# Attention kernel: row maxima split in transposed form, the high part of the turned rows on ScalarE, the lowest part of v on GpSimd, the maxima sent by SyncE

## The chip, the cores and the metric

The kernel runs on one core of a Trainium2 chip. That core has five engines with a program each: TensorE (PE, matmuls into PSUM), VectorE (DVE), ScalarE (ACT), GpSimd (POOL) and SyncE (SP, which here only issues DMAs). They wait for each other through semaphores. The metric is the device time of one execution in microseconds (us).

## The reference

For 8 batches of 512 tokens with 512 channels and 16 heads of 32:

```python
mod = (silu(c) @ wmod).reshape(8, 6, 1, -1)          # sa, ca, ga, sb, cb, gb
h = layernorm(x) * (1 + ca) + sa
q, k, v = split(h @ W_attn.T)                        # heads of 32
att = softmax(causal(q @ k.T) / sqrt(32)) @ v
x = x + ga * (att @ W_proj.T)
h = layernorm(x) * (1 + cb) + sb
x = x + gb * mlp(h)                                  # 512 -> 1024 -> 1024 -> 512, relu
```

## The kernel before, in words

`setup` computes the modulation, `attention` the softmax part for all batches, `mlp` the projection and the MLP. The change is in `attention` alone.

Full fp32 accuracy comes from split numbers: a value is written as a high part and a remainder, and three products of parts are added. So q and k have two parts each (`qk_parts`), h has two (`h_parts`), v three in bf16 (`v_parts`: columns D:2D high, 2D:3D middle, 0:D lowest).

**Slots and units.** The work of a batch is 8 slots (one per pair of heads, numbered 0 to 7), and a slot has 5 units (u = 0 to 4). In slot p all stages of different pairs run side by side, each some slots behind (`behind(b, p, lag, first)`; a lag beyond slot 0 falls into the next batch's first slots):
- lag 0: PE computes the scores of pair p by query (L758), DVE takes the row maxima (L653, L657);
- lag 1: the maxima of the pair before are transposed by PE in unit 1 (L808) and sent by DMA into two rows of `stack`, the operand of the second score matmuls;
- lag 2: PE computes the scores again, by key, with the maximum subtracted through those two rows (L770); ACT takes the exponential twice, to f16 (L529) and to f32 (L536); POOL (units 0, 1, 3, 4) and DVE (unit 2, L668) form the low part `prob_lo`;
- lag 3: PE multiplies with v (L790), DVE gathers (L639, L642);
- lag 4: POOL scales (L465), SP stores `o_rows` in odd slots (L424).

The first key matmul of a slot (unit 0) waits for `max_in` of its pair: the maxima that were turned one slot earlier have to be in `stack`.

**The linear work of the next batch** is dealt out over the units by the table WORK, from slot 4 of one batch to slot 3 of the next: four transposes of x (TURN, slot 4, units 0 to 3), eight q/k projections (QK 0 to 7), eight v units. QK 1 ends in slot 5 unit 4, QK 3 in slot 7 unit 0, QK 5 in slot 1 unit 3, QK 7 in slot 2 unit 4. After each of these four SP issues 12 DMAs of 128 KB, which lay `qk_parts` out into `stack` (L398, a "group" below). Two PSUM banks alternate over all linear units; `lin_act` counts what ACT has taken from them and `lin_taken` what DVE has taken.

**Order.** Each engine's order is fixed by the code: one in-order stream per engine, `slot(b, p, ...)` for each slot, batch 0 and batch 7 written out and batches 1 to 6 in a loop. On ACT, a unit is: exponentials, then in unit 1 the copy of the turned maxima (L543) and their two DMA issues (L546), then the linear item. On SP: linear item's group, then (unit 1, odd slots) the store.

**The maxima before.** DVE forms -max rounded to fp32r (L676, `neg_max[..., 0, :]`) and its remainder (L679) at the end of the slot, on 128 x 8 elements; PE turns both at once into 16 rows of 128; ACT copies these 16 rows to `max_rows` (two buffers) and issues two DMAs of 4 KB.

Of the kernel before, what the change touches and what calls it, by code (L numbers as in the profile page):

```python
# [294 lines left out]
def attention(nc, mem, x, wqkv, ident, mask_qk, mask_kq, ident_bf, mod_cols, attn_dram):  # L295
# [16 lines left out]
    neg_max = mem.sb("neg_max", [P, 2, 2, 2 * NT])  # L312
    max_rows = mem.sb("max_rows", [4 * NT, 2, P], F32R)
# [13 lines left out]
    lin_done, lin_act, h_hi, lin_taken = (mem.sem(n) for n in ("lin_done", "lin_act", "h_hi", "lin_taken"))  # L327
    v_mid_ready, v_split = (mem.sem(n) for n in ("v_mid_ready", "v_split"))
    stack_in = [mem.sem(f"stack_in{g}") for g in range(GROUPS)]
    score_done, score_taken, max_hi, max_ready, turn_done, turn_taken = (  # L330
        mem.sem(n) for n in ("score_done", "score_taken", "max_hi", "max_ready", "turn_done", "turn_taken"))
# [16 lines left out]
    def v_no(n, g, t):  # L348

        return V_UNITS * n + NT * g + t  # L350

# [31 lines left out]
    with nc.Block() as block:  # L383
        @block.sync
        def _(sp):
# [46 lines left out]
        def _(pool):  # L432
# [15 lines left out]

            def slot(b, p, first, more):
                for u in range(UNITS):  # L450
# [18 lines left out]
                    if p == 2 and u == 4 and more:  # L469
                        inverse_deviation(b + 1)  # L470
# [4 lines left out]
        def _(act):  # L475
            act.sem_inc(prob_ready, KEY_CREDITS)
            act.sem_inc(turn_taken, 1)

            def modulate(n, c):
# [39 lines left out]
            def slot(b, p, first, more):  # L519
                for u in range(UNITS):  # L520
# [18 lines left out]
                    if u == 1 and turned:  # L539

                        n, q = turned
                        act.wait_ge(turn_done, PAIRS * n + q + 1)
                        nc.scalar.copy(max_rows[:, q % 2, :], turn_bank[0:4 * NT, 0:P]).then_inc(turn_taken, 1)  # L543
                        act.wait_ge(turn_taken, 1 + PAIRS * n + q + 1)
                        for part in range(2):
                            act.dma_start(  # L546
                                f32(stack[3 * D + part:3 * D + part + 1, 0, 2 * q:2 * q + 2, :]),
                                f32(max_rows[2 * NT * part:2 * NT * (part + 1), q % 2, :]))\
                                .then_inc(max_in[q], 16)
# [6 lines left out]
        def _(dve):  # L556
# [38 lines left out]
            def v_rest(n, g, t):  # L595

                hs = slice(g * H // 2, (g + 1) * H // 2)
                dve.wait_ge(v_split, V_CREDITS + v_no(n, g, t) - 1)
# [3 lines left out]

            def v_lowest(n, g, t):
                hs = slice(g * H // 2, (g + 1) * H // 2)
                rest = heads(full[:, ORDER.index((V, g, t)) % 2, 0:C // 2])
                dve.wait_ge(v_mid_ready, v_no(n, g, t) + 1)
                nc.vector.tensor_tensor(v[:, t, hs, 0:D], rest, v[:, t, hs, 2 * D:3 * D],
                                        ALU.subtract).then_inc(v_split, 1)
# [12 lines left out]
            def step_after_item(n, item):  # L621

                if item[0] == V and last_item(item):
                    v_lowest(n, item[1], item[2])

# [3 lines left out]
            for item in before_first():  # L629
                after_item(0, item)  # L630
                step_after_item(0, item)
# [12 lines left out]
            def slot(b, p, first, more):  # L644
                for u in range(UNITS):
# [14 lines left out]
                    if not (first and p == u == 0):  # L660
                        earlier = (work(b, p, u - 1, more) if u else work(b, p - 1, UNITS - 1, more) if p
                                   else [(b, item) for item in WORK[PAIRS - 1][UNITS - 1]])
                        for n, item in earlier:
                            step_after_item(n, item)
# [7 lines left out]
                    if p < PAIRS and u == UNITS - 1:  # L672

                        dve.wait_ge(score_taken, SCORE_CREDITS + unit_no(b, p, UNITS))
                        peak = row_max[:, p % 2].rearrange("p h t -> p (h t)")
                        nc.vector.tensor_scalar_mul(neg_max[:, p % 2, 0, :].bitcast(F32R), peak, -1.0)\  # L676
                            .then_inc(max_hi, 1)
                        dve.wait_ge(max_hi, PAIRS * b + p + 1)
# [14 lines left out]
        def _(pe):  # L693
# [69 lines left out]
            def scores_by_key(b, p, u):  # L763

                bank = key_bank[(UNITS * p + u) % 2]
                if u == 0:
                    pe.wait_ge(max_in[p], 32 * (b + 1))
# [27 lines left out]
            def slot(b, p, first, more):  # L795
                for u in range(UNITS):
# [469 lines left out]
```

## Time and profile before

| | |
|---|---|
| time, median of 3 runs | 1666.01 us (1664.12 to 1668.75) |
| the profiled execution | 1668.86 us, its span 1667.1 us, mean granted PE clock 0.972 |
| busy: PE, DVE, ACT, POOL | 1536.4 us (92%), 1000.6 (60%), 644.2 (39%), 370.6 (22%) |
| attention | from about 60 to 780 us |
| MLP | from about 780 us to the end |

Shares are over the whole span and average two parts with different limits. In the profile, L12 is line 12 of the kernel; SPq and ACTq are the DMA issues of these engines, with the time that an issue occupies them. The granted clock is a fraction of 2.4 GHz. Idle time of an engine is put down to what ended it.

### The profile page before, as it was taken

The page shows a single profiled execution, that of the slowest core. Times are in us where ns is not written, and L with a number is a line of the kernel's source. Part 1 is how long each engine was busy: PE and PEld are TensorE (multiplying, and loading weights), DVE is VectorE, ACT ScalarE, POOL GpSimd, SP SyncE. Part 2 cuts the span into 40 slices and gives each one's busy share as a digit, 9 for nine tenths or more (in the row PEclk, how much of TensorE's full clock was granted, in tenths as well). Part 3 has the DMA queues.
Part 4 walks back from the last instruction along what each step waited for, and adds up shares of the span by engine and source line. Part 5 has one row for each costly group of instructions (what it writes and reads, how often), then busy time and mean ns, then how long its engine had stood idle before and what let it go on. Part 6 is the DMA issues. An engine that isn't in the chain of part 4 may idle for free.

```text
span 1667.1 us, 33396 instructions
## 1 busy us (share of the span) xinstructions
PE 1536.4 (92%) x12032; PEld 1345.7 (81%) x12032; DVE 1000.6 (60%) x2287; ACT 644.2 (39%) x1346; POOL 370.6 (22%) x360
## 2 busy tenths in 40 slices
PE   5499989898989898985699999999999999999998
PEld 1377777787777777874699999999999999999998
DVE  2477878878788878773844444445444454444442
ACT  2146666666666666674512122121212122121211
POOL 0224555454555554553000000000000000000000
PEclk9699999999999999996799999999999999999999
DMA  5162534243425252423600111001100011011100
GB/s 227 43 162 62 127 73 123 71 120 76 121 69 134 58 135 62 110 71 112 204 26 20 45 45 45 13 31 44 44 30 27 31 44 44 0 51 37 44 14 13
DMA packets 75272, 116.98 MB, mean 70 GB/s; under 512 B 10568, under 2 KB 27976, under 8 KB 74704
## 3 DMA queue, kind: packets, MB, share of 16 engines
q1 hardware_dynamic: 68816, 107.31, 23.4%
q10 hardware_dynamic: 6400, 8.92, 1.5%
q8 instruction: 36, 0.59, 0.1%
q14 instruction: 20, 0.16, 0.0%
HBM read 48.52 MB, written 16.81 MB: 39 GB/s over the span
## 4 chain that ended last, share of the span: by engine, by line
PE 51%; DVE 1%; DMA 1%; SPq 0%; ACT 0%; issue 0%; POOL 0%; DVEq 0%; POOLq 0%
PE feature L1203 33%; PE token L1184 16%; PE feature L1174 1%; PE token L1165 1%; DVE w L1115 1%; DMA b_rows<-b 0%; DMA w_ring<-wproj_t 0%; DVE y L1069 0%; SPq L945 0%; DVE y L1067 0%; ACT w L1021 0%; DVE attn_tiles L1093 0%; POOL mlp_rstd L982 0%; DVE gated L1077 0%; DVE res_tiles L1080 0%
## 5 line engine op out<-in xcount | busy, mean ns | idle before, releaser
L454 POOL TENSOR_TENSOR prob_lo<-prob,prob_hi 128x512 f16<-128x512 f32 x256 | 302.0, 1183 | 362.0 <-ACT prob L536 361.0
L1203 PE MATMUL feature<-y,w 128*128 128x256 f32 x3072 | 377.5, 284 | 5.1 <-DVE w L1115 5.1
L1203 PEld LDWEIGHTS feature<-y,w 128*128 128x128 f32 x3072 | 374.2, 190 | 6.7 <-DVE w L1115 5.3
L1015 ACT ACTIVATE mlp_full<-feature,b_cols 128x256 f32<-128x256 f32 x256 | 120.4, 476 | 647.0 <-PE feature L1203 617.4
L1067 DVE CAST y<-mlp_full 128x256 fp32r<-128x256 f32 x256 | 75.2, 294 | 302.4 <-ACT mlp_full L1015 302.1
L529 ACT ACTIVATE prob_hi<-key_score 128x512 f16<-128x512 f32 x320 | 192.3, 601 | 143.0 <-PE key_score L770 140.9
L708 PE MATMUL lin<-h_parts,wqkv 128*128 128x512 f32 x768 | 215.1, 403 | 9.5 <-DVE h_parts L585 9.5
L1203 PEld LDWEIGHTS feature<-turned,w 128*128 128x128 f32 x1536 | 189.2, 191 | 5.1 <-DVE w L1115 3.8
L1203 PE MATMUL feature<-turned,w 128*128 128x256 f32 x1536 | 189.7, 284 | 3.4 <-DVE turned L1069 3.4
L536 ACT ACTIVATE prob<-key_score 128x512 f32<-128x512 f32 x320 | 192.4, 601 | 0.0
L982 POOL TENSOR_TENSOR mlp_rstd<-mlp_var_eps,mlp_minus_half 128x2 f32<-128x2 f32 x16 | 11.1, 696 | 799.3 <-DVE mlp_var_eps L1088 799.3
L1184 PE MATMUL token<-w,y 128*128 128x512 f32 x768 | 183.6, 398 | 0.0
L657 DVE TENSOR_REDUCE row_max<-score 128x1 f32<-128x512 f32 (+2 forms) x384 | 181.0, 501 | 3.5 <-PE score L758 3.3
L1184 PEld LDWEIGHTS token<-w,y 128*128 128x128 f32 x768 | 143.4, 188 | 33.7
L708 PEld LDWEIGHTS lin<-h_parts,wqkv 128*128 128x128 f32 x768 | 140.2, 192 | 36.6 <-DVE h_parts L585 11.4
L758 PE MATMUL score<-stack 96*128 96x512 f32 (+3 forms) x512 | 155.0, 364 | 2.4 <-DMA stack<-qk_parts 2.4
L770 PE MATMUL key_score<-stack 98*128 98x512 f32 (+3 forms) x512 | 142.9, 341 | 0.0
L790 PEld LDWEIGHTS o_bank<-v_parts,prob_hi 128*128 128x128 f16 x1280 | 100.5, 99 | 27.4 <-issue 23.2
L790 PE MATMUL o_bank<-v_parts,prob_hi 128*128 128x97 bf16 x1280 | 117.4, 212 | 4.3 <-POOL prob_lo L454 2.8
L790 PE MATMUL o_bank<-v_parts,prob_lo 128*128 128x65 bf16 x1280 | 114.5, 196 | 0.0
L1069 DVE TENSOR_TENSOR y<-mlp_full,y 128x256 fp32r<-128x256 f32 x256 | 109.0, 426 | 8.8
L716 PE MATMUL lin<-wqkv,h_parts 128*128 128x256 f32 x768 | 107.7, 285 | 0.0
(95 smaller groups left out, 1902.8 us busy)
## 6 DMA issues: line engine op xcount, KB each, us to landing
stack<-qk_parts SPq DMA_DIRECT2D x384, 128.0 KB, 2.4
x_tiles<-x SPq DMA_DIRECT2D x32, 256.0 KB, 3.1
attn_dram<-o_rows SPq DMA_DIRECT2D x32, 256.0 KB, 2.2
attn_tiles<-attn_dram SPq DMA_DIRECT2D x16, 512.0 KB, 4.4
res_tiles<-x SPq DMA_DIRECT2D x16, 512.0 KB, 3.6
out<-res_tiles ACTq DMA_DIRECT2D x16, 512.0 KB, 2.8
wmod_sb<-wmod SPq DMA_DIRECT2D x4, 1536.0 KB, 16.4
w_ring<-w_t SPq DMA_DIRECT2D x12, 512.0 KB, 6.2
```

Of the source, the lines that this page charges most:

```text
L454: nc.gpsimd.tensor_tensor(prob_lo[:, key[1] % 2, u, :], prob[:, u, :], prob_hi[:, key[1] % 2, u, :], ALU.subtract).then_inc(lo_pool, 1)
L529: nc.scalar.activation(prob_hi[:, q % 2, u, :], bank[:], ACT.Exp, scale=SOFTMAX_SCALE, bias=P_SHIFT)
L536: nc.scalar.activation(prob[:, u, :], bank[:], ACT.Exp, scale=SOFTMAX_SCALE, bias=P_SHIFT)\
L657: last = nc.vector.reduce_max(row_max[:, p % 2, hh, t:t + 1], bank[:, col:col + P * (t + 1)], AX.X)
L708: mm = nc.tensor.matmul(lin_bank_of((QK, f))[:], wqkv[:, wl, c, at:at + P], h[:, hl, c, :], start=(c == 0 and k == 0), stop=(c == NC_ - 1 ...
L758: mm = nc.tensor.matmul(bank[:, col:col + n], stack[0:3 * D, 0, head, t * P:(t + 1) * P], stack[0:3 * D, 1, head, 0:n], start=False, stop= ...
L770: mm = nc.tensor.matmul(bank[:, col:col + n], stack[0:3 * D + 2, 1, head, t * P:(t + 1) * P], stack[0:3 * D + 2, 0, head, t * P:T], start= ...
L790: mm = nc.tensor.matmul(o_bank[:, i * VW + low:(i + 1) * VW], part[:, p % 2, u, at:at + P], v[:, j, head, low:VW], start=(j == 0 and part ...
L1015: nc.scalar.activation(full[:, f % 2, :], fbank[f % 4][:, 0:CH], ACT.Relu, bias=bias[:, f:f + 1])\
L1069: nc.vector.tensor_tensor(dst[:, 1, c, :], full[:, ring, :], f32(dst[:, 0, c, :]), ALU.subtract)\
L1184: mm = nc.tensor.matmul(bank[:], data[:, dl, c, t * P:(t + 1) * P], weights[:, wl, c, :], start=(c == 0 and i == 0), stop=(c == chunks - 1 ...
L1203: mm = nc.tensor.matmul(fbank[f % 4][:, 0:CH], weights[:, wl, c, f * P:(f + 1) * P], data[:, dl, c, :], start=(c == 0 and i == 0), stop=(c ...
```

## The change

- **Maxima.** PE turns the plain maxima (8 rows) as soon as `score_taken` allows. ACT writes the negated, rounded rows (`max_rows[:, 0, :]`), DVE forms the remainder from the same PSUM bank in unit 2, after its prob_lo and its linear item, into `max_rows[:, 1, :]`. SP issues the two DMAs in unit 2. `max_rows` has one buffer, so ACT waits for the DMAs of the pair before.
- **Turned rows of h.** ACT applies the modulation twice, to `full` and, as fp32r, to the high part of `h_parts`; the cast on DVE goes. The PSUM bank is then free after ACT, and PE's wait is changed to `lin_act` where the bank's last user was a TURN.
- **v.** The lowest part is computed by POOL, right after the linear item's unit, and no longer by DVE one unit later. DVE's next use of the `full` buffer waits for it.

```diff
         @block.sync (in slot, each unit)
                     for n, item in work(b, p, u, more):
                         after_item(n, item)
+                    turned = behind(b, p, 1, first)
+                    if u == 2 and turned:
+                        n, q = turned
+                        wait_apart(sp, turn_taken, 1 + PAIRS * n + q + 1, (o_out[0], 16))
+                        for part in range(2):
+                            sp.dma_start(f32(stack[3 * D + part:3 * D + part + 1, 0, 2 * q:2 * q + 2, :]),
+                                         f32(max_rows[:, part, :])).then_inc(max_in[q], 16)
                     done = behind(b, p, 4, first)
...
         @block.gpsimd
+            def v_lowest(n, item):
+                if item[0] != V or not last_item(item):
+                    return
+                g, t = item[1:3]
...
+                pool.wait_ge(v_mid_ready, v_no(n, g, t) + 1)
+                nc.gpsimd.tensor_tensor(v[:, t, hs, 0:D], rest, v[:, t, hs, 2 * D:3 * D], ALU.subtract)\
+                    .then_inc(v_split, 1)
...
+                    for n, item in work(b, p, u, more):
+                        v_lowest(n, item)
                     if p == 2 and u == 4 and more:
...
         @block.scalar
-                nc.scalar.activation(full[:, c % 2, :], lin_bank_of((TURN, c))[:], ACT.Identity,
-                                     scale=mod_now[:, NC_ + c:NC_ + c + 1], bias=mod_now[:, c:c + 1])\
-                    .then_inc(lin_act, 1)
+                if c >= 2:
+                    act.wait_ge(lin_taken, LIN_CREDITS + lin_no(n, (TURN, c - 2)) + 1)
+                for made in (full[:, c % 2, :], h[:, 0, c, :]):
+                    last = nc.scalar.activation(made, lin_bank_of((TURN, c))[:], ACT.Identity,
+                                                scale=mod_now[:, NC_ + c:NC_ + c + 1], bias=mod_now[:, c:c + 1])
+                last.then_inc(lin_act, 1)
...
                         act.wait_ge(turn_done, PAIRS * n + q + 1)
-                        nc.scalar.copy(max_rows[:, q % 2, :], turn_bank[0:4 * NT, 0:P]).then_inc(turn_taken, 1)
-                        act.wait_ge(turn_taken, 1 + PAIRS * n + q + 1)
-                        for part in range(2):
-                            act.dma_start(
...
+                        act.wait_ge(max_in[(q - 1) % PAIRS], 32 * (n + 1 if q else n))
+                        nc.scalar.activation(max_rows[:, 0, :], turn_bank[0:2 * NT, 0:P], ACT.Copy, scale=-1.0)\
+                            .then_inc(max_hi, 1)
...
         @block.vector
             def split_h(n, c):
-                nc.vector.tensor_copy(h[:, 0, c, :], full[:, c % 2, :]).then_inc(h_hi, 1)
-                dve.wait_ge(h_hi, NC_ * n + c + 1)
...
-            def v_lowest(n, g, t):
...
-                        nc.vector.tensor_scalar_mul(neg_max[:, p % 2, 0, :].bitcast(F32R), peak, -1.0)\
...
+                    turned = behind(b, p, 1, first)
+                    if u == 2 and turned:
+
+                        n, q = turned
+                        dve.wait_ge(max_hi, PAIRS * n + q + 1)
                         nc.vector.scalar_tensor_tensor(
-                            out=neg_max[:, p % 2, 1, :].bitcast(F32R), in0=peak, scalar=-1.0,
-                            in1=neg_max[:, p % 2, 0, :], op0=ALU.mult, op1=ALU.subtract).then_inc(max_ready, 1)
+                            out=max_rows[:, 1, :], in0=turn_bank[0:2 * NT, 0:P], scalar=-1.0,
+                            in1=f32(max_rows[:, 0, :]), op0=ALU.mult, op1=ALU.subtract).then_inc(turn_taken, 1)
...
         @block.tensor
-                    pe.wait_ge(lin_taken, lin_no(n, unit_of(item)) + 1)
+                    place = ORDER.index(unit_of(item))
+                    if ORDER[place - 2][0] == TURN:
+                        pe.wait_ge(lin_act, lin_no(n, unit_of(item)) - 1)
+                    else:
+                        pe.wait_ge(lin_taken, lin_no(n, unit_of(item)) + 1)
...
-                        pe.wait_ge(max_ready, PAIRS * n + q + 1)
+                        pe.wait_ge(score_taken, SCORE_CREDITS + unit_no(n, q, UNITS))
                         pe.wait_ge(turn_taken, PAIRS * n + q + 1)
-                        nc.tensor.transpose(turn_bank[0:4 * NT, 0:P],
-                                            neg_max[:, q % 2, :, :].rearrange("p l m -> p (l m)"), ident[:])\
+                        nc.tensor.transpose(turn_bank[0:2 * NT, 0:P],
+                                            row_max[:, q % 2].rearrange("p h t -> p (h t)"), ident[:])\
                             .then_inc(turn_done, 1)
```

SP's order before, in the loop, from the group of QK 1 (end of slot 5) to the store of slot 7:

```order
L398 DMA stack<-qk_parts 32x2x512 [waits lin_taken]
L398 DMA stack<-qk_parts 32x2x512 x11
L393 REGISTER_ALU
L398 DMA stack<-qk_parts 32x2x512 [waits lin_taken]
L398 DMA stack<-qk_parts 32x2x512 x11
L58 REGISTER_ALU [waits o_out0]
L424 ISA [waits o_scaled]
L424 DMA attn_dram<-o_rows 128x4x128
```

SP's order after, at the same place:

```order
L403 DMA stack<-qk_parts 32x2x512 [waits lin_taken]
L403 DMA stack<-qk_parts 32x2x512 x11
L58 REGISTER_ALU [waits o_out0]
L428 DMA stack<-max_rows 1x8x128 [waits turn_taken]
L428 DMA stack<-max_rows 1x8x128
L398 REGISTER_ALU
L403 DMA stack<-qk_parts 32x2x512 [waits lin_taken]
L403 DMA stack<-qk_parts 32x2x512 x11
L436 ISA [waits o_scaled,o_out0]
L436 DMA attn_dram<-o_rows 128x4x128
L58 REGISTER_ALU [waits o_out0]
L428 DMA stack<-max_rows 1x8x128 [waits turn_taken]
```

The maxima of pair 5 (slot 6) now stand behind the first group, those of pair 6 (slot 7) behind the second group and the store.

DVE's order before, in slot 7 of the loop, unit 2 and the start of unit 3 (`full` is the remainder of a v unit):

```order
L657 TENSOR_REDUCE row_max<-score 128x1 [waits score_done]
L668 TENSOR_TENSOR prob_lo<-prob,prob_hi 128x512 [waits prob_ready]
L613 REGISTER_ALU
L598 ISA [waits lin_act]
L600 TENSOR_TENSOR full<-lin,v_parts 128x256 [waits v_split]
L651 REGISTER_ALU
```

DVE's order after, at the same place:

```order
L671 TENSOR_REDUCE row_max<-score 128x1 [waits score_done]
L677 TENSOR_TENSOR prob_lo<-prob,prob_hi 128x512 [waits prob_ready]
L633 REGISTER_ALU
L627 TENSOR_TENSOR full<-lin,v_parts 128x256 [waits lin_act]
L686 SCALAR_TENSOR_TENSOR max_rows<-turn,max_rows 8x128 [waits max_hi]
L665 REGISTER_ALU
```

The low part of the maxima is now made in unit 2, behind prob_lo and the linear item.

## Rows read from the trace of the kernel before

**Rows 1.** Windows, one batch: us, each engine's busy us, granted clock, DMA share, GB/s

```profile
235.80:321.80 86.00, 79.14 (x745) 65.42 (x744) 69.39 (x160) 55.36 (x117) 43.92 (x42) 1.00 0.40 99
```

**Rows 2.** Waits of PE in that batch: total us, times, longest us

```profile
PE lin L700 <- DVE h_parts L585: 2.5, 2, 1.3
PE lin L708 <- DVE h_parts L585: 1.6, 1, 1.6
PE score L743 <- DVE row_max L653: 0.9, 1, 0.9
PE score L743 <- DVE row_max L657: 0.8, 1, 0.8
PE key_score L748 <- ACT prob L536: 0.7, 2, 0.5
PE turn L808 <- DVE neg_max L679: 0.3, 1, 0.3
```

**Rows 3.** Groups by line, 60 to 915 us: busy us, mean ns, idle before

```profile
L465 POOL TENSOR_TENSOR o_rows<-o_sum,o_rcp 128x256 f32<-128x256 f32 x64 | 43.1, 673 | 4.1 <-DVE o_rcp L642 4.1
...
L607 DVE TENSOR_TENSOR v_parts<-full,v_parts 128x256 bf16<-128x256 f32 x64 | 32.7, 511 | 1.0 <-ACT v_parts L497 1.0
...
L484 ACT ACTIVATE full<-lin,mod_now 128x512 f32<-128x512 f32 x32 | 25.3, 791 | 39.5 <-PE lin L700 37.8 <-DVE v_parts L607 1.7
...
L676 DVE TENSOR_SCALAR neg_max<-row_max 128x8 fp32r<-128x8 f32 x64 | 23.7, 370 | 0.9
...
L583 DVE CAST h_parts<-full 128x512 fp32r<-128x512 f32 x32 | 22.2, 694 | 17.0 <-ACT full L484 17.0
L679 DVE SCALAR_TENSOR_TENSOR neg_max<-row_max,neg_max 128x8 fp32r<-128x8 f32 x64 | 20.2, 316 | 2.2
```

**Rows 4.** The tile max_rows, its DMA issues: ns min/median/max, first and last start

```profile
L546 ACTq DMA_DIRECT2D stack<-max_rows x128: 627/629/1242, 99.2 to 759.1; - x128
```

**Rows 5.** Timeline of ACT, start of slot 4: start us, us, idle before

```profile
298.76 0.59 ACT L529 ACTIVATE prob_hi<-key_score 128x512 f16<-128x512 f32 x1
299.24 0.59 ACT L536 ACTIVATE prob<-key_score 128x512 f32<-128x512 f32 x1
```

**Rows 6.** Timeline of PE, first key matmuls of slots 5, 7 and 0

```profile
311.06 0.40 PE L770 MATMUL key_score<-stack 98*128 98x512 f32 x1
...
329.88 0.40 PE L770 MATMUL key_score<-stack 98*128 98x512 f32 x1
...
339.36 0.40 PE L770 MATMUL key_score<-stack 98*128 98x512 f32 x1
```

**Rows 7.** DMA issues by line: KB each, median us to landing

```profile
stack<-qk_parts SPq DMA_DIRECT2D x384, 128.0 KB, 2.4
...
c_sb<-c_t SPq DMA_DIRECT2D x1, 16.0 KB, 2.0
```

**Rows 8.** Timeline of DVE, slot 6, unit 2

```profile
326.87 0.69 DVE L668 TENSOR_TENSOR prob_lo<-prob,prob_hi 128x512 f16<-128x512 f32 x1 [0.99 <-ACT prob L536]
327.48 0.68 DVE L589 TENSOR_TENSOR qk_parts<-lin,qk_parts 128x512 fp32r<-128x512 f32 x1
```

**Rows 9.** Timeline of SP, groups of QK 1 and QK 3 and the store

```profile
321.87 7.98 SPq L398 DMA_DIRECT2D stack<-qk_parts  x12
...
333.03 7.74 SPq L398 DMA_DIRECT2D stack<-qk_parts  x12
341.02 0.39 SPq L424 DMA_DIRECT2D attn_dram<-o_rows  x1
```

**Rows 10.** Windows, columns as in rows 1

```profile
386.00:391.70 5.70, 3.16 (x33) 2.21 (x31) 3.64 (x8) 4.21 (x9) 3.31 (x3) 1.00 0.01 1
391.70:395.20 3.50, 3.19 (x31) 2.70 (x28) 3.46 (x7) 2.06 (x5) 1.24 (x1) 0.51 0.00 0
...
825.20:832.00 6.80, 6.12 (x28) 6.12 (x29) 5.92 (x10) 5.24 (x12) 0.00 (x0) 0.50 0.77 251
```

**Rows 11.** Timeline of PE in the MLP

```profile
825.88 1.01 PE L1203 MATMUL feature<-y,w 128*128 128x256 f32 x3 [5.09 <-DVE w L1115]
```

More of the change, by code:

```diff
@@ L311, in attention @@
     row_max = mem.sb("row_max", [P, 2, 2, NT])
-    neg_max = mem.sb("neg_max", [P, 2, 2, 2 * NT])
-    max_rows = mem.sb("max_rows", [4 * NT, 2, P], F32R)
+    max_rows = mem.sb("max_rows", [2 * NT, 2, P], F32R)
     prob = mem.sb("prob", [P, UNITS, 512])
@@ L326, in attention @@
         mem.sem(n) for n in ("aggr_done", "var_ready", "rstd_ready", "x_norm", "mod_ready"))
-    lin_done, lin_act, h_hi, lin_taken = (mem.sem(n) for n in ("lin_done", "lin_act", "h_hi", "lin_taken"))
+    lin_done, lin_act, lin_taken = (mem.sem(n) for n in ("lin_done", "lin_act", "lin_taken"))
     v_mid_ready, v_split = (mem.sem(n) for n in ("v_mid_ready", "v_split"))
     stack_in = [mem.sem(f"stack_in{g}") for g in range(GROUPS)]
-    score_done, score_taken, max_hi, max_ready, turn_done, turn_taken = (
-        mem.sem(n) for n in ("score_done", "score_taken", "max_hi", "max_ready", "turn_done", "turn_taken"))
+    score_done, score_taken, max_hi, turn_done, turn_taken = (
+        mem.sem(n) for n in ("score_done", "score_taken", "max_hi", "turn_done", "turn_taken"))
     max_in = [mem.sem(f"max_in{p}") for p in range(PAIRS)]
@@ L350, in v_no, with v_before @@
         return V_UNITS * n + NT * g + t
+    def v_before(g, t):
+        place = ORDER.index((V, g, t))
+        return max([NT * o[1] + o[2] + 1 for i, o in enumerate(ORDER[:place]) if o[0] == V and (place - i) % 2 == 0],
+                   default=0)
     def unit_no(b, p, u):
@@ L447, in _ @@
             pool.wait_ge(ones_ready, 2)
+            def v_lowest(n, item):
+                if item[0] != V or not last_item(item):
+                    return
+                g, t = item[1:3]
+                hs = slice(g * H // 2, (g + 1) * H // 2)
+                rest = full[:, ORDER.index((V, g, t)) % 2, 0:C // 2].rearrange("p (h d) -> p h d", d=D)
+                pool.wait_ge(v_mid_ready, v_no(n, g, t) + 1)
+                nc.gpsimd.tensor_tensor(v[:, t, hs, 0:D], rest, v[:, t, hs, 2 * D:3 * D], ALU.subtract)\
+                    .then_inc(v_split, 1)
+            for item in before_first():
+                v_lowest(0, item)
             def slot(b, p, first, more):
@@ L477, in _ @@
             act.sem_inc(turn_taken, 1)
+            act.sem_inc(max_in[PAIRS - 1], 32)
             def modulate(n, c):
@@ L542, in slot @@
                         act.wait_ge(turn_done, PAIRS * n + q + 1)
-                        nc.scalar.copy(max_rows[:, q % 2, :], turn_bank[0:4 * NT, 0:P]).then_inc(turn_taken, 1)
-                        act.wait_ge(turn_taken, 1 + PAIRS * n + q + 1)
-                        for part in range(2):
-                            act.dma_start(
-                                f32(stack[3 * D + part:3 * D + part + 1, 0, 2 * q:2 * q + 2, :]),
-                                f32(max_rows[2 * NT * part:2 * NT * (part + 1), q % 2, :]))\
-                                .then_inc(max_in[q], 16)
+                        act.wait_ge(max_in[(q - 1) % PAIRS], 32 * (n + 1 if q else n))
+                        nc.scalar.activation(max_rows[:, 0, :], turn_bank[0:2 * NT, 0:P], ACT.Copy, scale=-1.0)\
+                            .then_inc(max_hi, 1)
                     for n, item in work(b, p, u, more):
@@ L597, in v_rest @@
                 hs = slice(g * H // 2, (g + 1) * H // 2)
-                dve.wait_ge(v_split, V_CREDITS + v_no(n, g, t) - 1)
+                before = v_before(g, t)
+                if before:
+                    dve.wait_ge(v_split, V_CREDITS + V_UNITS * n + before)
                 rest = heads(full[:, ORDER.index((V, g, t)) % 2, 0:C // 2])
@@ L601, in v_rest @@
                                         ALU.subtract).then_inc(lin_taken, 1)
-            def v_lowest(n, g, t):
[L604 to L608, printed above, removed]
             def after_item(n, item):
@@ L619, in after_item @@
                     v_rest(n, item[1], item[2])
-            def step_after_item(n, item):
-                if item[0] == V and last_item(item):
-                    v_lowest(n, item[1], item[2])
             row_stats(0, range(NT))
@@ L630, in _ @@
                 after_item(0, item)
-                step_after_item(0, item)
             def gather_output(n, q, hh):
@@ L659, in slot @@
                         last.then_inc(score_taken, 1)
[L660 to L664, printed above, removed]
                     key = behind(b, p, 2, first)
@@ L671, in slot @@
                         after_item(n, item)
-                    if p < PAIRS and u == UNITS - 1:
-                        dve.wait_ge(score_taken, SCORE_CREDITS + unit_no(b, p, UNITS))
-                        peak = row_max[:, p % 2].rearrange("p h t -> p (h t)")
-                        nc.vector.tensor_scalar_mul(neg_max[:, p % 2, 0, :].bitcast(F32R), peak, -1.0)\
-                            .then_inc(max_hi, 1)
-                        dve.wait_ge(max_hi, PAIRS * b + p + 1)
+                    turned = behind(b, p, 1, first)
+                    if u == 2 and turned:
+                        n, q = turned
+                        dve.wait_ge(max_hi, PAIRS * n + q + 1)
                         nc.vector.scalar_tensor_tensor(
-                            out=neg_max[:, p % 2, 1, :].bitcast(F32R), in0=peak, scalar=-1.0,
-                            in1=neg_max[:, p % 2, 0, :], op0=ALU.mult, op1=ALU.subtract).then_inc(max_ready, 1)
+                            out=max_rows[:, 1, :], in0=turn_bank[0:2 * NT, 0:P], scalar=-1.0,
+                            in1=f32(max_rows[:, 0, :]), op0=ALU.mult, op1=ALU.subtract).then_inc(turn_taken, 1)
                     if more and (p, u) == (1, 1):
@@ L766, in scores_by_key @@
                 if u == 0:
-                    pe.wait_ge(max_in[p], 32 * (b + 1))
+                    pe.wait_ge(max_in[p], (64 if p == PAIRS - 1 else 32) + 32 * b)
                 for _, hh, t, col in (r for r in BY_KEY if r[0] == u):
```

## The prediction

> **What bounds the kernel now.** I read in this order: busy shares by stage, the waits of one batch, then the issue queue of SyncE (SP) and the matmuls that start each slot. The kernel has two parts: attention, until about 780 us, and the MLP, which the change does not touch. In attention the work repeats with a period of 86.0 us per batch. The batch from 235.8 to 321.8 us stands for all of them: TensorE (PE) is busy for 79.14 of 86.00 us, VectorE (DVE) for 69.39, ScalarE (ACT) for 55.36 and GpSimd (POOL) for 43.92, at full granted clock [rows 1]. So PE sets the time. PE's own waits in that batch are short [rows 2]: 2.5 + 1.6 us in slot 4, where the turned x goes through ACT and DVE, 0.9 + 0.8 us on row maxima, 0.7 us on exponentials. Anything the change takes from ACT or DVE can give back no more than these. Anything that makes PE wait longer adds in full, since PE runs in order.
>
> **The relief.** The two DVE operations that make neg_max cost 370 and 316 ns, 64 times each; on DVE the eight v_parts subtractions of a batch (511 ns) and the four h_parts casts (694 ns) go too [rows 3]. That frees per batch about 8 x 0.69 + 8 x 0.51 + 4 x 0.69 = 12.4 us of DVE, less 8 new operations on 8 x 128 elements that read PSUM; no row shows one, and I take 0.3 us, as the 128 x 8 form (316 ns); the other end is the 511 ns of a form twice as wide. Net 10 us. ACT loses two issues of 0.63 us per pair [rows 4], 10 us per batch, and gains four modulating activations of 0.79 us [rows 3], 3.2 us. POOL gains eight subtractions, of about 0.67 us (its o_rows on 128 x 256 [rows 3]), with twice that as the other end: 5 to 11 us on an engine idle for 42 us. Their consumers are two v units (about 6 us) or a batch part away, so I charge nothing; if POOL's order is late once per batch, PE sees perhaps 1 us.
>
> What does PE get of it? Outside slot 4 it waits 2.7 us per batch with the neg_max wait [rows 2], and I credit half, 1.3 us, because the loop described below becomes nearly as long as the slots. Bounds: 0 and 2.7. In slot 4 the gain looks larger: PE may take the third and fourth bank after ACT instead of after DVE. But ACT's work is now longer there. From the end of its first exponentials (299.83 [rows 5]) it has three double modulations (3 x 1.58), two pairs of exponentials (2 x 1.07, as 298.76 to 299.83), and some 0.7 for the copy of the maxima and the starts: 307.4. DVE then splits turn 2 (0.7) and, after it in its order, the maxima (0.3); with the DMA (2.65, below) the maxima are there at 311.05. PE's first key matmul of slot 5 is at 311.06 now [rows 6]. So the 4.1 us of slot 4 turn into a wait for the maxima: credit 0 (bounds 0 and 3).
>
> **The path of the maxima.** Before, DVE prepares both parts, PE turns them in unit 1, ACT copies and issues two DMAs at once. After, DVE makes the low part in unit 2, behind its prob_lo and whatever linear item is there, and SP issues. From the DVE end to the landing: first issue to second 0.65 us [rows 4], plus landing. No row has a landing for this transfer; the nearest are 2.0 us (16 KB) and 2.4 us (128 KB) [rows 7]; I take 2.0, so 2.65, upper bound 3.05. In slots 5 to 7 prob_lo of unit 2 ends 2.32 us before the next slot's first key matmul (327.56 against 329.88 in slot 6 [rows 6, 8]). It comes earlier because ACT no longer issues two DMAs (1.3 us) just ahead of the exponentials behind it, but PE's key scores of unit 2 limit that: I take 0.4, bounds 0 and 1.3. In slot 5, where nothing else is in the way, the maxima then land 0.3 + 2.65 - 0.4 - 2.32 = **0.2 us** too late (bounds 0 and 1.0). Slots 0 to 4 are longer than 5 to 7, and I take them at nothing; half a microsecond in each of four is possible.
>
> **The queue of SP**, the main term. SP issues twelve stack loads per group, and they take the queue for 7.98 and 7.74 us [rows 9]. Two of the four groups fall just ahead of a send of maxima, in the fixed order of SP.
> - Slot 6: the first group runs from 321.87 to 329.85 [rows 9]. The maxima of pair 5 are ready on DVE by about 328.5 (prob_lo to 327.56, then the qk_parts item to 328.16 [rows 8]), but SP reaches them at 329.9. Landed: 329.9 + 0.65 + 2.0 = 332.55. PE needs them at 329.88 [rows 6]. PE waits **2.7 us**. SP's first load of the group hangs on slot 5's work alone, so this is not softened by earlier waits.
> - Slot 7: the second group starts 333.03 - 329.88 = 3.15 us after the slot's first key matmul, because its last linear item follows that matmul on PE; it moves with the stall. It ends at 340.76, the store of o_rows ends at 341.41 [rows 9], then the maxima of pair 6: 341.5 + 2.65 = 344.15, against 339.36 [rows 6]. PE waits **4.8 us**.
> - The groups sent at the ends of slots 1 and 2 end before DVE has the next maxima; cost 0.
>
> The row says that a DMA issue occupies SP for 0.65 us and everything behind it waits. The Trainium skill (DMA: Bandwidth & Descriptors, Rules for kernel authors) says that spreading DMAs over the engines only saves sequencer issue time. Read as a price, it would make this move a matter of 1.3 us of issue per pair, outside PE's path, and the total would be that of rival A. It holds for bandwidth; it leaves out that the queue is shared with twelve others.
>
> Sum per batch: 2.7 + 4.8 + 0.2 - 1.3 = 6.4 us. Seven batches have such loads inside the loop (the first loads lie before it): 7 x 6.4 = 45 us.
>
> **The clock.** Pauses of PE are followed here by half clock: a pause of 5.09 us ended at 825.88 [rows 11], and 825.2 to 832.0 ran at 0.50 [rows 10]; with PE busy for 3.16 of 5.70 us, the next 3.5 us ran at 0.51 (0.5 is 1.2 GHz, 1.0 is 2.4). A pause of 4.8 us per batch, 9.5 us after one of 2.7, may bring 3.4 to 6.8 us at half clock in slot 0, costing half of that: 1.7 to 3.4 us. In slot 7 the cost is hidden behind SP. That it falls at each such pause is open: slot 4's waits of 4.1 us brought it in one batch of the seven only, the one of that stretch. Bounds 0 and 7 x 3.4 = 24; I take **10 us**.
>
> Total: profiled execution 1668.86 (span 1667.1) + 45 + 10 = 1724. That execution lies 2.85 us above the median 1666.01, so on the median's basis: **1721 us**.
>
> **Rivals.**
> A. Faster. This would need the maxima to land before PE asks. It turns on one place, SP at the end of the group in slots 6 and 7: the group would have to be over 2.7 and 4.8 us sooner, that is, an issue would have to cost under 0.42 and 0.25 us instead of 0.65. For it: the store of o_rows issues in 0.39 us [rows 9]. Against: both groups of twelve there take over 7.7 us [rows 9]. Then the relief remains: 7 x (2.7 + part of slot 4's 4.1, say 0.5) = 22 us less: 1644. Decides from where the landing comes before the key matmul.
> B. No change: the sends hide as before and slot 4 and the relief cancel with the loop: about 1666.
> C. Only one of the two stalls comes, the one in slot 7, because PE's delay there makes the next group's data late enough for SP to send the maxima of slot 6 in time (not in the written order): 7 x (4.8 + 0.2 - 1.3) = 26: 1692 without the clock.
> D. The clock falls after every pause, and landing takes 2.4 us: 45 + 7 x 2 x 0.4 + 24 = 75: 1741; if no relief arrives either, 1750.
>
> **Chances.** My forecast 0.65, D 0.2, C 0.08, A 0.04, B 0.03. The range goes from C's 1692 to just short of D's end, 1748. About 0.3% (5 us) is what a measurement of this kernel tells from no change. Slower by more than that: forecast, C and D, 0.93; within: 0.03; faster: 0.04.
>
> **What would show it.** Right: the waits of PE's key_score matmuls name the max_rows DMA from SP, once in slot 7 and once in slot 0 of each batch, 2.7 and 4.8 us; SP's max_rows rows stand directly behind a group of twelve (and the store); the batch takes about 93 us; ACT's and DVE's busy time in attention falls, POOL's rises by 40 to 70 us. Wrong: no key_score wait on that DMA, or issues much shorter than 0.65 us. If the waits come in every slot with 1 to 2 us, then the DVE path and not the queue is the cause. If PE waits on v_parts, POOL's new work is. The MLP must take the same time as before.

## The result, and the profile after

The changed kernel takes 1729.68 us (median of 4 runs, 1728.95 to 1732.55), the kernel before beside it 1667.38. The ratio is 1.0378, 95% interval 1.0354 to 1.0401. All runs compared here and below are in the same, faster state. Forecast were 1721 us and a range of 1692 to 1748. The profiled execution took 1728.95 us, its span is 1727.2 us against 1667.1.

The windows of one batch, from one start of QK 1's group to the next (us, busy us of PE, PEld, DVE, ACT, POOL, granted clock, DMA share, GB/s), answer to [rows 1]. The second row is the beginning of a slot 0:

```profile
524.00:617.80 93.80, 82.74 (x743) 68.16 (x741) 60.48 (x138) 57.43 (x120) 48.17 (x49) 0.95 0.37 90
...
550.00:556.80 6.80, 6.17 (x24) 5.13 (x24) 1.12 (x3) 3.10 (x7) 2.50 (x4) 0.50 0.48 155
```

The batch takes 93.80 us instead of 86.00, though DVE is busy for 8.9 us less and ACT for 2.1 more (issues are not counted as busy). PE's busy time grew by 3.6 us without more work: the clock is 0.95 instead of 1.00.

The waits of PE over attention (total us, times, longest) show a wait, the first line, that did not exist before:

```profile
PE key_score L781 <- DMA stack<-max_rows: 69.0, 35, 5.0
PE lin L707 <- DVE x_tiles L606: 23.3, 1, 23.3
PE score L754 <- DVE row_max L671: 15.4, 17, 1.1
```

The new and moved groups of instructions answer to [rows 3] (busy us, mean ns, idle before). POOL's subtraction takes 683 ns, the modulation 766, DVE's new operation 271:

```profile
L468 POOL TENSOR_TENSOR v_parts<-full,v_parts 128x256 bf16<-128x256 f32 x64 | 43.7, 683 | 75.1 <-ACT v_parts L528 74.9
L515 ACT ACTIVATE h_parts<-lin,mod_now 128x512 fp32r<-128x512 f32 x32 | 24.5, 766 | 0.0
...
L686 DVE SCALAR_TENSOR_TENSOR max_rows<-turn,max_rows 8x128 fp32r<-8x128 f32 x63 | 17.1, 271 | 0.0
```

SP's timeline over slots 5 to 0 answers to [rows 9] (start us, us that the issues occupy the queue):

```profile
520.93 1.35 SPq L428 DMA_DIRECT2D stack<-max_rows  x2
524.90 7.86 SPq L403 DMA_DIRECT2D stack<-qk_parts  x12
532.88 1.43 SPq L428 DMA_DIRECT2D stack<-max_rows  x2
539.49 7.75 SPq L403 DMA_DIRECT2D stack<-qk_parts  x12
547.50 0.40 SPq L436 DMA_DIRECT2D attn_dram<-o_rows  x1
548.02 1.45 SPq L428 DMA_DIRECT2D stack<-max_rows  x2
```

DVE had these maxima earlier, at 530.96 in slot 6 and 544.33 in slot 7 (timeline of DVE):

```profile
530.69 0.27 DVE L686 SCALAR_TENSOR_TENSOR max_rows<-turn,max_rows 8x128 fp32r<-8x128 f32 x1
...
544.06 0.27 DVE L686 SCALAR_TENSOR_TENSOR max_rows<-turn,max_rows 8x128 fp32r<-8x128 f32 x1
```

And PE took its first key matmuls of slots 7 and 0 when the DMA had landed; they answer to [rows 6]:

```profile
535.46 0.50 PE L781 MATMUL key_score<-stack 98*128 98x512 f32 x1 [2.34 <-DMA stack<-max_rows]
...
550.63 0.79 PE L781 MATMUL key_score<-stack 98*128 98x512 f32 x1 [3.84 <-DMA stack<-max_rows]
```

Between DVE's end and SP's issue lie 1.92 us in slot 6 and 3.69 us in slot 7. In slots 0 to 5 of the same batch it is 0.03 us. From the first of the two issues to the matmul it is 2.47 to 2.61 us wherever PE waits.

Lengths of the slots of one batch, each from its first key matmul to the next slot's, in us. "e10" and "e9" are kernels of the experiments below, each in a batch without half clock: e10 is the change with SP's order mended, e9 has the split of the maxima one unit earlier as well. In brackets: how long the next slot's first key matmul is held by the maxima. A key matmul that is not held starts 0.32 us after the score matmul ahead of it, before that one has ended, so these numbers are about 0.16 us longer than the idle times in the rows.

| slot | before | after | e10 | e9 |
|---|---|---|---|---|
| 0 | 10.64 | 11.10 | 9.90 (0.3) | 9.44 |
| 1 | 10.14 | 10.19 | 10.25 | 10.16 |
| 2 | 11.19 | 11.18 | 11.18 | 11.18 |
| 3 | 11.90 | 12.62 (0.4) | 12.63 (0.4) | 12.23 |
| 4 | 13.87 | 11.61 (1.15) | 11.58 (1.15) | 11.01 |
| 5 | 9.41 | 9.53 | 9.53 | 9.49 |
| 6 | 9.41 | 11.96 (2.5) | 9.95 (0.5) | 9.41 |
| 7 | 9.48 | 15.17 (4.0) | 10.21 (0.6) | 9.48 |
| sum | 86.04 | 93.36 | 85.23 | 82.40 |

### The profile page after: what moved, and what is told of

Read it like the earlier page. It is cut to its first block, busy times and chain, and to the rows that moved or that the text cites. A ratio compares the mean times of both kernels' runs of the same rounds, so it can differ in the third digit from the quotient of the medians.

```text
span 1727.2 us, 33443 instructions
## 1 busy us (share of the span) xinstructions
PE 1557.0 (90%) x12032; PEld 1362.2 (79%) x12032; DVE 927.9 (54%) x2127; ACT 666.3 (39%) x1378; POOL 407.2 (24%) x424
## 4 chain that ended last, share of the span: by engine, by line
PE 49%; DVE 1%; DMA 1%; ACT 0%; issue 0%; SPq 0%; POOL 0%; DVEq 0%; POOLq 0%
PE feature L1214 32%; PE token L1195 16%; PE feature L1185 1%; PE token L1176 1%; DVE w L1126 1%; DMA w_ring<-w_t 0%; DMA w_ring<-wproj_t 0%; ACT w L1032 0%; DVE wproj L1126 0%; DVE y L1080 0%; DVE attn_tiles L1104 0%; POOL mlp_rstd L993 0%; DVE gated L1116 0%; DVE gated L1118 0%; DVE res_tiles L1091 0%
## 5 line engine op out<-in xcount | busy, mean ns | idle before, releaser
L479 POOL TENSOR_TENSOR prob_lo<-prob,prob_hi 128x512 f16<-128x512 f32 x256 | 298.4, 1166 | 310.8 <-ACT prob L567 309.8
L715 PE MATMUL lin<-h_parts,wqkv 128*128 128x512 f32 x768 | 220.5, 411 | 0.2 <-ACT h_parts L515 0.2
L781 PE MATMUL key_score<-stack 98*128 98x512 f32 (+3 forms) x512 | 153.3, 363 | 69.0 <-DMA stack<-max_rows 69.0
L715 PEld LDWEIGHTS lin<-h_parts,wqkv 128*128 128x128 f32 x768 | 143.7, 196 | 26.9 <-ACT h_parts L515 0.6
L781 PEld LDWEIGHTS key_score<-stack 98*128 98x128 f32 x512 | 87.5, 201 | 81.1 <-DMA stack<-max_rows 79.7
L723 PE MATMUL lin<-wqkv,h_parts 128*128 128x256 f32 x768 | 115.8, 300 | 0.0
L723 PEld LDWEIGHTS lin<-wqkv,h_parts 128*128 128x128 f32 x768 | 111.0, 207 | 4.8 <-issue 0.9
```

The lines of the kernel that those rows point to most:

```text
L479: nc.gpsimd.tensor_tensor(prob_lo[:, key[1] % 2, u, :], prob[:, u, :], prob_hi[:, key[1] % 2, u, :], ALU.subtract).then_inc(lo_pool, 1)
L715: mm = nc.tensor.matmul(lin_bank_of((QK, f))[:], wqkv[:, wl, c, at:at + P], h[:, hl, c, :], start=(c == 0 and k == 0), stop=(c == NC_ - 1 ...
L723: mm = nc.tensor.matmul(lin_bank_of((V, g, t))[:, 0:C // 2], h[:, hl, c, t * P:(t + 1) * P], wqkv[:, wl, c, at:at + C // 2], start=(c == 0 ...
L781: mm = nc.tensor.matmul(bank[:, col:col + n], stack[0:3 * D + 2, 1, head, t * P:(t + 1) * P], stack[0:3 * D + 2, 0, head, t * P:T], start= ...
```

## Experiments

Each was run side by side with the kernel before, whose median was 1669.8 us beside e1 to e4, 1668.7 beside e5, e6, e7 and e9, and 1668.5 beside e10 to e13. Where two kernels of different groups are compared below, the difference of the medians and that of the ratios lie up to 3 us apart. Theory Q is the queue of SP, rival D the later split on DVE. "Group" is the twelve stack loads of one pair of q/k projections.

| run | us | ratio to before (95%) |
|---|---|---|
| e1: both groups behind the maxima | 1697.3 | 1.0167 (1.0149 to 1.0186) |
| e2: before, SP sends | 1723.7 | 1.0325 (1.0306 to 1.0343) |
| e3: before, h and v parts moved | 1660.2 | 0.9950 (0.9933 to 0.9967) |
| e4: e1 with the split in unit 1 | 1654.0 | 0.9901 (0.9880 to 0.9923) |
| e5: before, h part alone | 1666.7 | 0.9985 (0.9971 to 0.9998) |
| e6: before, v part alone | 1659.8 | 0.9947 (0.9931 to 0.9963) |
| e7: after, split in unit 1 | 1706.4 | 1.0228 (1.0207 to 1.0248) |
| e9: e4 with x behind | 1637.1 | 0.9824 (0.9801 to 0.9846) |
| e10: e1 with x behind | 1667.4 | 0.9998 (0.9986 to 1.0011) |
| e11: e10, QK 1's group in front | 1690.7 | 1.0138 (1.0118 to 1.0159) |
| e12: e10, QK 3's group in front | 1738.4 | 1.0414 (1.0394 to 1.0434) |
| e13: e9 without the h part | 1651.0 | 0.9893 (0.9874 to 0.9912) |

**e2: the queue alone.** The kernel before; only the issuing engine differs.

```diff
 (ScalarE, unit 1)
-                        act.wait_ge(turn_taken, 1 + PAIRS * n + q + 1)
-                        for part in range(2):
-                            act.dma_start(...)
 (SyncE, unit 1, behind the linear item)
+                        wait_apart(sp, turn_taken, 1 + PAIRS * n + q + 1, (o_out[0], 16))
+                        for part in range(2):
+                            sp.dma_start(...)
```

> The kernel before, with one edit: SyncE instead of ScalarE issues the two DMAs of the maxima, in unit 1 of the slot, behind ScalarE's copy. Split, transpose and linear work as before. Theory Q: waits of 2.7 us (slot 7) and 4.8 us (slot 0) in seven batches, 52 us, plus about 10 us of clock, less what ScalarE's 10 us per batch bring (0 to 10): about 1720 us (1705 to 1735). Rival D: the maxima leave as early as before, so 1667 us or a little less. A rival that prices the issue alone (1.3 us on an engine that is idle) expects no more than 1667 either.

Measured 1723.7 us, 3.25% slower: 54 of the 62 us come back with the smallest part of the change, although ACT had the maxima ready as early as before (in slot 6 its copy ends 5.6 us before the next slot's first key matmul would need it, both here and in the kernel before). SP's timeline and PE's two matmuls in one batch:

```profile
525.99 7.86 SPq L398 DMA_DIRECT2D stack<-qk_parts  x12
533.98 1.43 SPq L423 DMA_DIRECT2D stack<-max_rows  x2
540.45 7.77 SPq L398 DMA_DIRECT2D stack<-qk_parts  x12
548.34 1.43 SPq L423 DMA_DIRECT2D stack<-max_rows  x2
```

```profile
536.56 0.50 PE L773 MATMUL key_score<-stack 98*128 98x512 f32 x1 [2.40 <-DMA stack<-max_rows]
...
550.92 0.53 PE L773 MATMUL key_score<-stack 98*128 98x512 f32 x1 [3.02 <-DMA stack<-max_rows]
```

Rival D cannot act here, and neither can the price of the issue alone.

**e1: the groups moved out of the way.** The changed kernel, with SP's order altered in two slots.

```diff
                     for n, item in work(b, p, u, more):
-                        after_item(n, item)
+                        if item not in HELD_BACK:          # QK 1 and QK 3
+                            after_item(n, item)
...
                                          f32(max_rows[:, part, :])).then_inc(max_in[q], 16)
+                    if u == 2 and p in HELD_UNTIL and more:   # slots 6 and 7
+                        after_item(b + 1, HELD_UNTIL[p])
```

> The changed kernel, with one edit on SyncE: the groups of twelve stack loads of QK 1 and QK 3 are sent after the maxima of slots 6 and 7 instead of before them. Theory Q (the maxima wait in SP's queue behind these groups): the waits of 2.5 and 4 to 5 us at the starts of slots 7 and 0 (18.6 + 30.3 us in the trace of the changed kernel) go, and the half-clock stretches behind them; a wait of 0.2 to 0.9 us per slot from the longer way through DVE stays. 1729.7 - 49 - about 10 + 7 = about 1678 us (1668 to 1690). Rival D (the later split on DVE delays the maxima in every slot, wherever SP's groups stand): at most 15 us are won, 1715 us or more.

Measured 1697.3 us: 32 us won of the 52 expected. The waits at the starts of slots 7 and 0 went down to 0.5 and 0.6 us, but a new one stood at the start of slot 1. QK 3's group now ran into slot 0, then came the four loads of x, and then the maxima, whose DMA took 3.9 us from issue to matmul instead of 2.6:

```profile
527.66 7.76 SPq L403 DMA_DIRECT2D stack<-qk_parts  x12
536.16 1.92 SPq L393 DMA_DIRECT2D x_tiles<-x  x4
538.23 1.43 SPq L432 DMA_DIRECT2D stack<-max_rows  x2
```

```profile
542.17 0.80 PE L787 MATMUL key_score<-stack 98*128 98x512 f32 x1 [3.75 <-DMA stack<-max_rows]
```

So the expectation failed on its size, and the reason looks like the same mechanism one slot later. e10 tests that.

**e10: x behind the maxima too.** In slot 0 the loads of x are issued in unit 2, behind the send.

> The changed kernel (split in unit 2) with SyncE's order alone mended: both groups of stack loads behind the maxima of slots 6 and 7, and in slot 0 the loads of x behind the maxima. Theory Q: of the run that held the groups only (1697) the wait at the start of slot 1, 3.5 to 4.3 us in six batches, goes, with the half clock behind it: about 1665 us (1660 to 1672). What remains against the kernel before is the later split, 0.4 to 1.2 us in four slots. Rival: the group held back to slot 0 delays something else, 1680 us or more.

Measured 1667.4 us, no different from the kernel before. Reordering SP alone took away all 62 us. What is left is waits of 0.3 to 1.15 us at the starts of five slots, from the later split, and the relief of DVE and ACT. They cancel here; e9 below puts a number on each.

**e11 and e12: one group in front again.** Each is e10 with one of the two groups back in its old place.

> As the run with both groups held and x behind, but the group of QK 1 stands ahead of the maxima of slot 6 again. Theory Q: one wait of 2.5 us instead of 0.5 at the start of slot 7, 14 us in seven batches, and up to 6 us of half clock: 15 to 20 us above the run with both held, about 1682 us. Rival C (the waits are not additive, the loop of the maxima absorbs the one): within 5 us of it.

> As the run with both groups held and x behind, but the group of QK 3 stands ahead of the maxima of slot 7 again, and only that of QK 1 is held. Theory Q by its arithmetic: the held group now starts about 1 us before the first key matmul of slot 7 and ends 6.8 us after it; QK 3's group starts then, instead of 3.15 us after, and ends 14.7 us after it; with the store and the maxima (3.2 us) they land at 17.9 us, against 9.6: a wait of about 8.3 us at the start of slot 0 in place of 4. So one group fewer ahead of the maxima brings nothing: about 1725 us (1712 to 1740). Rival (each group has its own price): about 1700 us.

e11: 1690.7 us, 23 us above e10 where 15 to 20 were expected. Slot 6 is 11.97 us instead of 9.95, and slot 7 is 11.40 instead of 10.21, in which no wait on the maxima grew: there the clock was halved for 3.4 us after the pause, in all seven batches, and in none of e10's. The windows after the first key matmul of slot 7 in e11 and in e10 (last columns: clock, DMA share, GB/s):

```profile
513.40:516.80 3.40, 3.40 (x13) 2.44 (x12) 1.07 (x3) 1.52 (x4) 1.73 (x2) 0.50 0.00 0
```

```profile
497.10:500.50 3.40, 3.40 (x41) 2.93 (x40) 1.39 (x4) 2.56 (x6) 2.19 (x3) 1.00 0.87 199
```

e12: 1738.4 us, slower than with both groups in front. The two groups run back to back and the maxima of slot 7 stand behind both:

```profile
533.83 1.30 SPq L429 DMA_DIRECT2D stack<-max_rows  x2
535.29 15.60 SPq L403 DMA_DIRECT2D stack<-qk_parts  x24
551.14 0.41 SPq L442 DMA_DIRECT2D attn_dram<-o_rows  x1
551.66 1.47 SPq L429 DMA_DIRECT2D stack<-max_rows  x2
```

```profile
554.29 0.79 PE L787 MATMUL key_score<-stack 98*128 98x512 f32 x1 [8.24 <-DMA stack<-max_rows]
```

The wait of 8.24 us was expected as 8.3, from the lengths in SP's queue. The total lies 13 us above the point expected and within its range; the half clock lasted 10.2 us around that pause in each batch, which would account for the excess. That a group has a fixed price of its own is refuted.

**e7 and e4: the split one unit earlier.** DVE's part of the maxima and SP's send stand in unit 1.

```diff
-                    if u == 2 and turned:
+                    if u == 1 and turned:
```

> The changed kernel, with the low part of the maxima in unit 1 instead of unit 2, SyncE's send in unit 1 as well, and the groups of stack loads where the change has them. Theory Q: the waits at the starts of slots 7 and 0 stay at 2.5 and 4 us (SP is late, not VectorE), those of 0.4 to 1.4 us in the other slots (20 us in all) go: about 1710 us (1700 to 1715). Rival D (VectorE's late split is the cause): 1655 us.

> The changed kernel with the groups held back as in e1 and the low part of the maxima made by VectorE in unit 1 (and sent by SyncE in unit 1) instead of unit 2. Theory Q with the loop: no wait of TensorE on the maxima anywhere; what is left is the relief of ScalarE and VectorE: 1635 to 1655 us. Rival: VectorE in unit 1 now waits for ScalarE's exponentials and hands its row maxima out later, which TensorE feels as waits on row_max: 1665 to 1690 us.

e7: 1706.4 us, as Q has it. The short waits in slots 3 and 4 went, the two of the queue stayed (2.5 and about 4 us). So of the changed kernel's time the split in unit 2 accounts for 23 us more, although the prediction took it at next to nothing. e4: 1654.0 us, within its range, but its expectation of no wait anywhere was wrong. A wait of 1.6 to 2.5 us remained in five batches, at the start of slot 1, where the loads of x stood ahead:

```profile
510.91 1.93 SPq L393 DMA_DIRECT2D x_tiles<-x  x4
512.98 1.46 SPq L432 DMA_DIRECT2D stack<-max_rows  x2
```

```profile
517.12 0.50 PE L787 MATMUL key_score<-stack 98*128 98x512 f32 x1 [2.10 <-DMA stack<-max_rows]
```

**e9: the best kernel.** e4, with the loads of x in slot 0 behind the maxima.

```diff
-                if p == 0 and more:
-                    wait_apart(sp, lin_done, lin_no(b, (TURN, NC_ - 1)) + 1, (o_out[0], 16))
-                    load_x(b + 1)
...
+                    if p == 0 and u == 1 and more:     # behind the send of the maxima
+                        wait_apart(sp, lin_done, lin_no(b, (TURN, NC_ - 1)) + 1, (o_out[0], 16))
+                        load_x(b + 1)
```

> As e4 (split and send in unit 1, two groups held back), and SyncE issues the four loads of x in slot 0 behind the maxima instead of ahead of them. In e4 the maxima of slot 0 left 2.4 us after VectorE had them and arrived 4.15 us after their issue instead of 2.6, because the loads of x stand ahead of them; TensorE waited 2 us per batch there. Theory Q: that wait goes, 7 x 1.9 = 13 us less than e4: about 1641 us. Rival (VectorE is late in slot 0 by itself, and something else ends the slot): 1650 to 1655 us.

Measured 1637.1 us, 1.8% faster than before and about 5.4% faster than the change as it was made. Between 398 and 490 us, over a batch, no wait of PE on the maxima is left:

```profile
PE score L760 <- DVE row_max L677: 2.1, 2, 1.1
PE score L760 <- DVE row_max L673: 0.9, 1, 0.9
PE o_bank L807 <- DVE o_rcp L662: 0.8, 1, 0.8
PE lin L713 <- ACT h_parts L521: 0.3, 1, 0.3
```

Beside e10, which differs by the unit of the split and of what SP issues behind it, e9 shows what the late split costs: 30 us, of which 2.8 us per batch (85.23 against 82.40). Beside the kernel before it shows what the relief is worth where nothing holds it back: 31 us, of which 3.6 us per batch.

**e3, e5, e6, e13: the linear parts.** e3 puts both the h and the v part into the kernel before, e5 and e6 one each. e13 takes the h part out of e9. The edits are the change's own.

> The kernel before, with two of the three parts of the change: ScalarE writes the high part of the turned rows (and TensorE's wait goes by ScalarE), GpSimd forms the lowest part of v. The maxima go their old way. Theory: the relief of VectorE (about 7 us per batch) is worth something only where TensorE waits: 4.1 us per batch in slot 4 and 2.4 us elsewhere, of which I expect 2 to 4 us without the loop of the maxima behind them: 1640 to 1655 us. Rival (GpSimd's place in the order or ScalarE's longer work in slot 4 turns into new waits): 1667 us or more.

> The kernel before, with one part of the change: ScalarE writes the high part of the turned rows. Theory: slot 4, where this acts, stays at 13.9 us, since ScalarE's longer work replaces VectorE's cast; the time stays within 4 us of the kernel before. Rival (TensorE's earlier bank pays): up to 4 us per batch, 1640 to 1655 us.

> The kernel before, with one part of the change: GpSimd forms the lowest part of v. Theory: VectorE's subtraction stood in front of work that ScalarE and TensorE wait for in slot 0 (10.6 us there before, 9.5 in the run with both parts), so this part alone gives nearly all of what both gave: 1.1 us x 7, 1658 to 1663 us. Rival: GpSimd's order delays v or the next turned rows: 1667 us or more.

> The kernel of e9 (1637 us) without one of the three parts: VectorE casts the high part of the turned rows again and TensorE waits for VectorE. In the old order this part was worth 0.15% (e5). Theory: in e9 the maxima leave early and slot 4 is bound by the turned rows (11.0 to 12.6 us), so now the part pays: slot 4 goes to about 13.3 us, 7 x 1 to 2 us, about 1648 us. Rival: it is worth as little as in e5, 1637 to 1640 us.

e3 gave 1660.2 us, a smaller gain than the 1640 to 1655 expected: slot 0 fell from 10.6 to 9.5 us, but slot 4 stayed at 13.8 to 14.4. e5 gave 1666.7 (0.15% less than before), e6 1659.8: the v part alone gives the gain of slot 0, and the h part nearly nothing.

The traces show what holds slot 4 in e3 and e5. PE's waits there did fall (in e3 to 3.0 us, from 4.4 in the batches before that ran at full clock), but in all seven batches of both kernels 3.4 or 6.8 us of the slot ran at half clock, against two of seven before. In e3 ACT's two DMA issues also still stand ahead of its second modulation. Batch 3 of e3, a window in the half clock and these rows of ACT:

```profile
389.90:393.20 3.30, 3.30 (x12) 2.67 (x10) 2.37 (x6) 3.30 (x7) 1.16 (x1) 0.50 0.00 0
```

```profile
384.77 1.30 ACTq L570 DMA_DIRECT2D stack<-max_rows  x2
386.18 0.78 ACT L508 ACTIVATE full<-lin,mod_now 128x512 f32<-128x512 f32 x1 [1.45 <-issue]
```

In e9 SP sends, ACT's second modulation starts 0.16 us after the start of its copy of the maxima instead of 1.68, and the half clock stands in two of seven slots 4. There the same h part is worth 14 us by the medians, 11 by the ratios (e13: 1651.0, expected 1648). In the profiled executions slot 4 gives about 9 us of it (12.6 instead of 11.0 us in batches without half clock; e13 too has the half clock in two of seven); where the rest comes from stays open. That the half clock and ACT's issues are what swallowed the part in e3 and e5 is read from these traces; no run separates the two. The value of a part hangs on what else holds the slot.

## Why the prediction was right, point by point

- **SP's queue, slot 6: 2.7 us.** Measured 2.5. The group took 7.86 us, and issue to matmul took 2.58 where 2.65 was worked out. Shown by e1, e2 and e11.
- **Slot 7: 4.8 us.** The slot grew by 5.7 us. The step "the cost is hidden behind SP" was wrong: at half clock PE ends QK 3 later, so the group started 4.03 us after the first key matmul instead of 3.15, and everything behind it moved by these 0.9 us. The wait that shows is shorter, 4.0 us (3.5 to 5.2 over the batches), since PE's own work, slower at half clock, filled the other 1.7.
- **Clock: 10 us.** The direction holds, the size was too small. The table's slot 0 has 11.10 us with 3.4 us of half clock from its start on, those of batches 3 and 5 have 12.3 with 6.8 us, against 9.44 in e9 with none. Over the seven slots 0 the excess above e9's is 15.6 us, to which slot 7's 0.9 us per batch come. The prediction also misread its evidence: slot 4's waits were followed by half clock in two batches of the seven before (0 and 3), not in one.
- **Slot 4: credit 0.** Wrong. The slot became 2.3 us shorter (13.87 to 11.61), within the bound of 3, and still ends in a wait of 1.15 us for the maxima. The loop described exists, but it is shorter than the prediction made it: that added ACT's operations at their full durations (3 x 1.58 and 2 x 1.07 us), while in the trace modulations start 0.66 us and exponentials 0.48 us apart, so this stretch of ACT takes 6.0 us instead of 7.6.
- **Relief elsewhere: 1.3 us, and the late split: 0.2 us.** In the changed kernel the relief lies in slot 0, 1.2 us, from v (e6), and the half clock took it back. Slot 3 lost 0.7 us, 0.4 of it a wait for the maxima. Both terms were mis-sized: slot 4 included, the relief is worth 3.6 us per batch (before against e9), and the late split costs 2.8 (e10 against e9). Their net, 0.8 us gained against 1.1 forecast, came out by luck, as two errors of nearly the same size cancelled. Either error alone, over seven batches, is 16 to 18 us.
- **Last batch: taken at nothing.** It costs 5.0 us from its slot 2 to the last store: slot 3 ends in a wait of 3.0 us for the maxima, behind the last group and a store in SP's queue, and slots 4 to 6, which have no linear work and were 7 to 8 us long, each end in one of 1.4 us.
- **GpSimd's new work: nothing.** Right: 683 ns each, and no wait of PE on v appears.
- **Sum.** From the first key matmul of slot 2 in batch 0 to that in batch 7 it was 600.7 us before and 657.7 after: 57.0 us, or 8.1 per batch, where 6.4 and the clock's 1.4 were forecast. With the last batch's 5.0 and 1.6 won at the start it is 60.4, against 60.1 between the spans. The main term is right in its mechanism and its size: SP's queue with the clock behind it was put at 7 x 7.5 + 10 = 62 us, and the changed kernel loses 62 us against e10, where only SP's order differs. Within it the waits came out smaller (2.5 and 4.0 us) and the clock dearer, so that the sum fits this well is partly luck too.

The rule of the Trainium skill that was weighed (DMA: Bandwidth & Descriptors, Rules for kernel authors: spreading DMAs over engines saves only issue time) holds in its words, as the engine that issues is all that differs in e2. But issue time stands in a queue: twelve issues are 7.9 us, and with 1.3 us of sends moved behind them the kernel lost 54 us.

## What to carry to other kernels

When a DMA moves to another engine's queue, list what is issued ahead of it there, with the time that each issue occupies, and compare the end of that list with the moment of need; an idle queue on average says nothing. Put small transfers that a matmul waits for ahead of bulk loads that are needed later: with SP's order mended the same change went from 3.8% slower to no difference (e10), and with the split one unit earlier as well to 1.8% faster (e9). And test a part of a change in the schedule where it will live, since the h part was worth 2 us in one and 11 to 14 in the other.

## What the runs showed of the hardware

- An issue of the stack loads (128 KB) occupied SP for 0.60 us in the median, one of the maxima (4 KB) SP for 0.67 and ACT for 0.63 us; a load of x (256 KB) took 0.35 and a store of o_rows (256 KB) 0.41 us. Single issues took longer, up to 2.1 us.
- With four loads of 256 KB issued just ahead of the 4 KB sends it was 3.6 to 4.3 us from issue to matmul (e1, six batches) and 3.2 to 4.2 us (e4, six batches), where 2.6 us is usual. In e10, with the loads of x behind and the rest of e1's order kept, it was 2.6 us.
- A pause of PE of 2.5 to 2.9 us was followed by 3.4 us at half clock in seven of seven batches of e11. Pauses of 3.5 to 5.2 us in the changed kernel were followed by 3.4 or 6.8 us, and those of 8.4 us in e12 stood beside 10.2 us, of which the beginning lies in the pause. In e10, with pauses of 0.3 to 1.4 us, none stood in the batches of the loop. But the longest pause does not decide it alone: in slot 4 of e3 and e5 no pause is above 1.7 us, three to five stand within 8 us, and the half clock came in seven of seven batches; in the kernel before, with pauses of 1.2 and 1.3 us there ahead of it and one of 1.6 us behind, in two.
